# Conditioned linear attention on one core: opening, seam, end of the state and last stretch put in another order

## The chip, the cores and the metric

The kernel runs on one core of a Trainium2 chip. The metric is the device time of one execution in microseconds (us), as the median of several runs; a profile of one execution stands beside it. Five engines matter: TensorE (PE, matmuls, with its weight loads shown apart as PEld), VectorE (DVE), ScalarE (ACT), GpSimd (POOL) and SyncE (SP, which here only issues transfers). Each engine takes its own instructions strictly in the order in which they are written, and waits on semaphores for the others.

## What is computed

Two batches (b) of 2048 tokens with 512 channels, 8 heads of 64. The reference, cut to what matters:

```python
xn = _ln(x, ln_w, ln_b)
q = xn @ Wq + bq
k = xn @ Wk + bk + (1.0 - src_mask) * -1000000.0
q = softmax(q per head, over the 64 channels)
k = softmax(k, over the 2048 tokens)
v = ((xn @ Wv + bv) * src_mask)
att = einsum('bnhd,bnhl->bhdl', k, v)
y = einsum('bnhd,bhdl->bnhl', q, att)
scale, shift = split(silu(emb) @ W_emb + b_emb)
hh = _ln(y, ln2_w, ln2_b) * (1.0 + scale) + shift
return x + silu(hh) @ W_out + b_out
```

## The kernel before

A batch is T = 16 tiles of 128 tokens; tile m of the output counts through both batches, so batch 1 has the tiles 16 to 31 (written T to 2T-1). The order of each engine is written out by hand, as a list of calls; nothing reorders it. Every large product is made from three fp32r matmuls (high by high, high by low, low by high; `split_product`), four blocks of them to a tile, twelve matmuls in all. So each operand is split first: ACT copies the high part, DVE or POOL subtracts it for the low part.

Stages, in order of time:

- **Opening and first batch, keys and queries.** For each tile PE turns the normalised x (`turn_z`, four transposes into one PSUM bank ZB), ACT copies the high part out (`zT_high`), DVE the low part (`zT_low`), PE forms `product_k` and `product_q`. DVE adds the bias to k and keeps a running maximum (`k_tile`, two instructions), adds the bias to q (`q_add`), takes the maximum of each head (`q_top`), POOL subtracts it (`q_shift`), ACT takes the exponential (`exp_q`). The statistics of x go by chunks of tiles, listed in XC: `x_tile_stats` for each tile, then `x_finish` for a chunk, a chain of some 13 tiny DVE instructions (a reciprocal root by Newton steps, in four parts 0 to 3); only then can ACT normalise the tiles of the chunk (`normalise_x`). Weights are split too (`wk_high`, `weight_low`), and biases are worked out by `key_bias`, `bias_parts`, `bias_sum`.
- **State** (`state_steps`): PE accumulates `product_g` over 16 tiles in four banks; ACT and DVE prepare exponentials and masked x (`exp_k`, `ek_high`, `zm_high`, `k_less_max`, `masked_z`, `zm_low`, `ek_low`). Afterwards `sum_exponentials` (sums of the keys' exponentials), `products_att`, `att_blocks` give the attention matrix.
- **Seam and second batch.** The keys and queries of batch 1 are made while batch 0 goes through `product_y` (PE), `y_tile` (DVE, reciprocal and scaling, it frees the PSUM for the next `product_y`), `y_raw` and `y_finish` (statistics by the chunks YC, in four parts as above), `normalise_y` (ACT), `turn_y` (PE), `scale_shift` (ACT: four scalings and a tanh), `silu` (DVE), `h_high` (ACT), `h_low` (POOL), `product_out` (PE), `out_tile` (DVE), store (SP). Outputs up to HT-1 = 11 are done here; 12 to 15 are held for the state and the last stretch.
- **State of batch 1**, then the **last stretch**: `product_y` of tiles 16 to 31, their norms and outputs.

Two rules of the last stretch matter. `product_y(m)` waits for `y_tile(m-1)`. `product_out(m)` waits for `h_low(m)` and, since there are two output banks, for `out_tile(m-2)`. On ACT the loop is `scale_shift(m)`, `normalise_y(m+1)`, `h_high(m)`.

## Time and profile before

| | us |
|---|---|
| median of 3 runs (496.40 to 498.42) | 497.97 |
| the profiled execution | 496.72 |
| its span in the trace | 494.9 |
| PE busy | 465.5 (94%) |
| DVE busy | 364.5 (74%) |
| ACT busy | 265.0 (54%) |
| POOL busy | 124.6 (25%) |

Busy PE time counts from the start of a matmul to its modelled end, so overlapping matmuls count once. 1.8 us of the execution lie outside the span. Times in the rows below are microseconds from the start of the span.

### The profile page before, as it was taken

How to read it: one execution, taken by the hardware profiler on the slowest of the kernel's cores; microseconds unless marked ns; L12 is line 12 of the kernel's file. 1: busy time of each engine (PE TensorE's matmuls, PEld its weight loads, DVE VectorE, ACT ScalarE, POOL GpSimd, SP SyncE). 2: the span in 40 equal slices, each digit the busy share in tenths (PEclk: the TensorE clock that was granted, in tenths of full speed). 3: DMA queues.
4: the chain of work that ended last, by engine and by line, in shares of the span. 5: the costliest groups of instructions: out<-in, count | busy, mean ns of one | idle time of the engine just before them, and what ended most of it. 6: DMA issues, size and time to landing. Idle time of an engine off the chain costs nothing.

```text
span 494.9 us, 7296 instructions
## 1 busy us (share of the span) xinstructions
PE 465.5 (94%) x2478; PEld 370.4 (75%) x2478; DVE 364.5 (74%) x893; ACT 265.0 (54%) x487; POOL 124.6 (25%) x106
## 2 busy tenths in 40 slices
PE   4988999998899989999999999998899988999997
PEld 1666876885688768778888888887678857877765
DVE  6699976765878766879677568667998538777762
ACT  4234332321787323347556556656979635477782
POOL 0013311120100000104223333223310131456565
PEclk9999999999999999999999999999999999999999
DMA  8991110112132210110203212121321000333344
GB/s 280 360 373 51 44 42 3 43 48 101 45 126 85 86 34 10 44 42 1 86 22 128 85 44 86 44 85 67 106 88 63 1 0 23 121 103 118 127 152 147
DMA packets 23093, 43.50 MB, mean 88 GB/s; under 512 B 1992, under 2 KB 2064, under 8 KB 23056
## 3 DMA queue, kind: packets, MB, share of 16 engines
q1 hardware_dynamic: 21968, 40.93, 24.4%
q10 hardware_dynamic: 1088, 2.10, 1.1%
q8 instruction: 20, 0.33, 0.3%
q14 instruction: 17, 0.14, 0.1%
HBM read 34.64 MB, written 8.39 MB: 87 GB/s over the span
## 4 chain that ended last, share of the span: by engine, by line
PE 76%; DVE 15%; ACT 4%; issue 4%; DMA 1%; POOL 1%; DVEq 0%; ACTq 0%
PE ps L1067 20%; PE ps L1069 20%; PE ps L1068 20%; PE ps L1072 8%; PE ps L1228 4%; PE ps L1160 1%; ACT ps L394 1%; DVE kf L816 1%; DVE res L843 1%; DVE xst_raw L615 1%; ACT x_in L308 1%; DVE qs L716 1%; ACT kf L382 1%; PE ps L1213 1%; PE ps L1132 1%
## 5 line engine op out<-in xcount | busy, mean ns | idle before, releaser
L561 POOL TENSOR_TENSOR qs<-qs,qmax 128x512 f32<-128x512 f32 x32 | 35.9, 1121 | 199.0 <-DVE qmax L721 199.0
L1067 PE MATMUL ps<-wk_hi,zT_hi 128*128 128x512 f32 x128 | 53.7, 420 | 2.0 <-DVE kf L702 2.0
L1067 PE MATMUL ps<-ek_hi,zm_hi 128*128 128x512 f32 x128 | 50.8, 397 | 2.9 <-DVE ek_lo L757 2.1
L293 ACT ACTIVATE zT_hi<-ps 128x512 fp32r<-128x512 f32 x32 | 19.1, 597 | 64.2 <-PE ps L1072 64.1
L1067 PE MATMUL ps<-wq_hi,zT_hi 128*128 128x512 f32 x128 | 52.5, 411 | 0.3 <-DVE qs L716 0.3
L1068 PE MATMUL ps<-wk_lo,zT_hi 128*128 128x512 f32 x128 | 51.0, 398 | 0.0
L1069 PE MATMUL ps<-wk_hi,zT_lo 128*128 128x512 f32 x128 | 50.8, 397 | 0.0
L1069 PE MATMUL ps<-wq_hi,zT_lo 128*128 128x512 f32 x128 | 50.6, 395 | 0.0
L1068 PE MATMUL ps<-wq_lo,zT_hi 128*128 128x512 f32 x128 | 50.5, 395 | 0.0
L1069 PE MATMUL ps<-ek_hi,zm_lo 128*128 128x512 f32 x128 | 49.9, 390 | 0.0
L1068 PE MATMUL ps<-ek_lo,zm_hi 128*128 128x512 f32 x128 | 49.9, 390 | 0.0
L574 POOL TENSOR_TENSOR res<-res,bo_all 128x512 f32<-128x512 f32 x32 | 42.1, 1320 | 20.0 <-DMA res<-in_x_dram 10.7
L716 DVE TENSOR_TENSOR qs<-ps,bq_all 128x512 f32<-128x512 f32 x32 | 22.1, 689 | 32.0 <-PE ps L1069 29.9
L702 DVE SCALAR_TENSOR_TENSOR kf<-ps,pen,bk_all 128x512 f32<-128x512 f32 x32 | 23.9, 745 | 13.5 <-PE ps L1069 13.5
L695 DVE TENSOR_TENSOR zT_lo<-ps,zT_hi 128x512 fp32r<-128x512 f32 x32 | 21.9, 686 | 13.7 <-ACT zT_hi L293 13.7
L1067 PEld LDWEIGHTS ps<-ek_hi,zm_hi 128*128 128x128 f32 x128 | 24.0, 188 | 10.4 <-DVE ek_lo L757 3.6
L1067 PEld LDWEIGHTS ps<-wk_hi,zT_hi 128*128 128x128 f32 x128 | 24.4, 190 | 9.1 <-issue 3.4
L293 ACT ACTIVATE eqT<-ps 128x512 f32<-128x512 f32 x17 | 10.2, 600 | 38.2 <-PE ps L1072 38.2
L323 ACT ACTIVATE eq<-qs 128x512 f32<-128x512 f32 x32 | 20.0, 625 | 19.2 <-POOL qs L561 19.2
L747 DVE TENSOR_TENSOR zm_lo<-x_in,zm_hi 128x512 fp32r<-128x512 f32 x32 | 22.4, 701 | 10.4 <-PE ps L1069 9.4
L843 DVE TENSOR_TENSOR res<-ps,res 128x512 f32<-128x512 f32 x32 | 21.9, 683 | 10.8 <-PE ps L1069 7.2
L308 ACT ACTIVATE x_in<-x_in,x_shift,x_r 128x512 f32<-128x512 f32 x32 | 25.6, 806 | 6.9 <-DVE x_shift L647 6.9
(210 smaller groups left out, 1150.7 us busy)
## 6 DMA issues: line engine op xcount, KB each, us to landing
x_in<-in_x_dram SPq DMA_DIRECT2D x32, 512.0 KB, 3.5
res<-in_x_dram SPq DMA_DIRECT2D x32, 256.0 KB, 2.7
out_dram<-res SPq DMA_DIRECT2D x32, 256.0 KB, 2.0
y<-in_L_cond_Wk_dram ACTq DMA_DIRECT2D x2, 512.0 KB, 5.0
kf<-in_L_cond_Wq_dram ACTq DMA_DIRECT2D x1, 1024.0 KB, 7.8
eq<-in_L_cond_W_out_dram SPq DMA_DIRECT2D x1, 1024.0 KB, 9.1
wv_mod<-in_L_cond_Wv_dram SPq DMA_DIRECT2D x1, 1024.0 KB, 11.3
eq<-in_L_cond_W_emb_dram SPq DMA_DIRECT2D x4, 256.0 KB, 9.9
```

Source lines behind the costliest of these rows:

```text
L293: act.activation(o, i, ACT.Copy, scale=scale).then_inc(s[done], 1)
L308: act.activation(x_in[:, at, :], x_in[:, at, :], ACT.Identity, bias=x_shift[:, n:n + 1], scale=x_r[:, n:n + 1]).then_inc(s["z_ok"], 1)
L561: pool.tensor_tensor(q_heads, q_heads, qmax[:].unsqueeze(2).broadcast_to([P, H, DH]), ALU.subtract).then_inc(s["q_shift"], 1)
L574: pool.tensor_tensor(res[:, m % RR, :], res[:, m % RR, :], bo_all[:], ALU.add).then_inc(s["res_b"], 1)
L702: dve.scalar_tensor_tensor(out=kf[:, n, :], in0=ps[:, OB if m == 1 else KB, :], scalar=pen[:, m:m + 1], in1=bk_all[:], op0=ALU.add, op1=AL ...
L716: dve.tensor_tensor(qs[:], ps[:, TB if m == 1 else QB, :], bq_all[:], ALU.add).then_inc(s["q_sum"], 1)
L747: dve.tensor_tensor(zm_lo[:, n % LO, :], x_in[:, at, :], zm_hi[:, n % HI, :].bitcast(F32), ALU.subtract).then_inc(s["zm_lo_ok"], 1)
L843: dve.tensor_tensor(res[:, m % RR, :], o_bank(m), res[:, m % RR, :], ALU.add).then_inc(s["o_ok"], 1)
L1067: pe.matmul(o, a[0], bb[0], start=start, stop=False)
L1068: pe.matmul(o, a[0], bb[1], start=False, stop=False)
L1069: return pe.matmul(o, a[1], bb[0], start=False, stop=stop)
L1072: return pe.transpose(o, i, ident[0:i.shape[0], 0:i.shape[0]])
```

## The change

Nothing is computed in another way; instructions change places, one chunk of x's statistics is cut in two, one turn gets its own bank, and the last two tiles are normalised by DVE.

- **Opening.** The chunk (2, 6) of batch 0 becomes (2, 4) and (4, 6). The turn of tile 1 goes to bank YTB, so it needn't wait for the low part of tile 0; `normalise_x(0, 1)` and the turn move ahead of `product_k(0, 0)`; `key_bias(1)` ahead of the first turn. `turn_z(0, 2)` moves behind `product_q(0, 1)`. DVE's list is put in another order, and the masked scales (`x_masked`) go to the steps 10 to 15.
- **Seam and state.** `sum_exponentials` stands ahead of the last `product_g`, with ACT's copy of the sums ahead of the copies of g; the small products of the sums stand ahead of the attention products.
- **End of batch 1's loop and state.** `product_out(10)` ahead of the turn of the keys' maxima, `product_q(1, 15)` ahead of their spreading; `turn_y(13)` goes behind the second `product_g`; DVE's and ACT's lists follow.
- **Last stretch.** `product_out(12)` stands ahead of the attention products, `product_out(13)` and `(14)` between the first `product_y`. The tiles 18 and 19 are turned one step later, then two tiles at once; two `product_y` follow each of the outputs 16 and 17. DVE takes `silu` ahead of `out_tile`; the finishes of the last three chunks are cut in two halves.

```diff
-    XC = [[(0, 2), (2, 6), (6, 10), (10, 14), (14, 16)]] * 2
+    XC = [[(0, 2), (2, 4), (4, 6), (6, 10), (10, 14), (14, 16)], [(0, 2), (2, 6), (6, 10), (10, 14), (14, 16)]]
+    LATE = 2
...
+        def z_bank(m):
+            return ps[:, YTB if m == 1 else ZB, :]
...
             def state_steps(b, last=lambda n: None):
...
+                sums_out(b)
                 for j in (0, 2):
...
             normalise_x(0, 0)
+            normalise_x(0, 1)
             act.wait_ge(s["wk_in1"], 16)
             wk_high(2)
             zT_high(0, 0)
-            normalise_x(0, 1)
...
             for m in range(T + 2, 2 * T):
                 scale_shift(m)
-                if m + 1 < 2 * T:
+                if m + 1 < 2 * T - LATE:
                     normalise_y(m + 1)
                 h_high(m)
...
+            def normalise_late(m):
+                dve.wait_ge(s["y_norm"], nth_chunk(YC, m // T, m % T))
+                dve.tensor_scalar(y_of(m), y_of(m), y_r[:, m % SR:m % SR + 1], y_shift[:, m % SR:m % SR + 1],
+                                  ALU.mult, ALU.add).then_inc(s["yn_late"], 1)
...
             weight_low(wk_lo, wk_raw, wk_hi, "wk", 1)
+            weight_low(wk_lo, wk_raw, wk_hi, "wk", 2)
             zT_low(0, 0)
-            weight_low(wk_lo, wk_raw, wk_hi, "wk", 2)
             weight_low(wk_lo, wk_raw, wk_hi, "wk", 3)
             zT_low(0, 1)
+            weight_low(wq_lo, wq_raw, wq_hi, "wq", 0)
+            weight_low(wq_lo, wq_raw, wq_hi, "wq", 1)
+            x_tile_stats(0, 2)
+            x_tile_stats(0, 3)
+            weight_low(wq_lo, wq_raw, wq_hi, "wq", 2)
+            weight_low(wq_lo, wq_raw, wq_hi, "wq", 3)
+            x_finish(0, 1)
...
-            for f in range(NB):
-                weight_low(wq_lo, wq_raw, wq_hi, "wq", f)
-                x_tile_stats(0, 2 + f)
-            x_finish(0, 1)
...
             k_tile(0, 0)
+            x_tile_stats(0, 4)
+            x_tile_stats(0, 5)
             zT_low(0, 2)
+            k_tile(0, 1)
...
             q_add(0, 0)
             q_top(0, 0)
-            k_tile(0, 1)
...
-            x_part(0, 0)
+            x_finish(0, 2)
             q_add(0, 1)
             zT_low(0, 3)
             q_top(0, 1)
...
             q_top(0, 2)
+            x_part(0, 0)
             x_part(0, 1)
             x_part_end(0, 1)
-            x_masked(0, 0)
-            x_masked(0, 1)
             x_part_end(0, 2)
...
             state_steps(1, last_outputs)
+            out_tile(HT)
             att_blocks(1)
...
             silu(HT + 3)
             y_tile(T + 2)
             y_raw(T + 2)
-            out_tile(HT)
+            out_tile(HT + 1)
             y_tile(T + 3)
             y_raw(T + 3)
             silu(T)
             y_finish(T + 3)
+            out_tile(HT + 2)
             silu(T + 1)
-            out_tile(HT + 1)
             y_tile(T + 4)
             y_raw(T + 4)
-            out_tile(HT + 2)
-            y_tile(T + 5)
-            y_raw(T + 5)
-            y_tile(T + 6)
-            y_raw(T + 6)
             for m in range(T, 2 * T):
-                out_tile(m - 1)
                 if m + 2 < 2 * T:
                     silu(m + 2)
-                if m + 6 < 2 * T:
-                    y_finish(m + 6)
-                if m + 7 < 2 * T:
-                    y_tile(m + 7)
-                    y_raw(m + 7)
+                out_tile(m - 1)
+                if m >= T + 2 and m + 6 < 2 * T:
+                    y_finish(m + 6, (2, 3))
+                    if m + 6 == 2 * T - 1:
+                        for k in range(2 * T - LATE, 2 * T):
+                            normalise_late(k)
+                for k in (2 * m - T + 5, 2 * m - T + 6) if m < T + 2 else (m + 7,):
+                    if k < 2 * T:
+                        y_tile(k)
+                        y_raw(k)
+                        y_finish(k, (0, 1) if m >= T + 1 and k > T + 7 else range(4))
...
             key_bias(0)
+            key_bias(1)
             turn_z(0, 0)
-            key_bias(1)
+            turn_z(0, 1)
             product_k(0, 0)
-            turn_z(0, 1)
...
             key_bias(3)
+            product_k(0, 1)
             pe.wait_ge(s["wq_in"], 16)
             bias_parts(cols[:, LNB:LNB + NB], wq_raw, "bq_part")
-            product_k(0, 1)
             product_q(0, 0)
-            turn_z(0, 2)
...
             bias_sum("bq_ps")
             product_q(0, 1)
+            turn_z(0, 2)
...
             for n in range(T):
+                if n == T - 1:
+                    sum_exponentials(1)
                 product_g(1, n)
+                if n == 1:
+                    turn_y(HT + 1)
...
-            sum_exponentials()
+            product_out(HT)
             products_att(1)
...
             product_y(T)
             product_y(T + 1)
+            product_out(HT + 1)
             product_y(T + 2)
-            product_out(HT)
-            product_y(T + 3)
+            product_out(HT + 2)
             turn_y(T)
             turn_y(T + 1)
-            product_out(HT + 1)
+            product_y(T + 3)
+            product_out(HT + 3)
             product_y(T + 4)
-            product_out(HT + 2)
-            turn_y(T + 2)
-            product_y(T + 5)
-            product_out(HT + 3)
-            product_y(T + 6)
             for m in range(T, 2 * T):
                 product_out(m)
-                if m + 3 < 2 * T:
-                    turn_y(m + 3)
-                if m + 7 < 2 * T:
-                    product_y(m + 7)
+                for k in ((m + 2,), (m + 2,), (m + 2, m + 3))[m - T] if m < T + 3 else (m + 3,):
+                    if k < 2 * T:
+                        turn_y(k)
+                for k in (2 * m - T + 5, 2 * m - T + 6) if m < T + 2 else (m + 7,):
+                    if k < 2 * T:
+                        product_y(k)
```

## Rows read from the trace of the kernel before

**Rows 1.** Busy time by stretch of the span, all engines, granted clock, DMA share.

```profile
core 0: us, PE busy (x) PEld busy (x) DVE busy (x) ACT busy (x) POOL busy (x), PEclk, DMA share, GB/s
12.00:27.00 15.00, 13.48 (x56) 8.91 (x56) 10.58 (x33) 5.07 (x9) 0.00 (x0) 1.00 1.03 363
27.00:45.00 18.00, 16.76 (x78) 12.92 (x76) 16.40 (x45) 7.00 (x14) 4.41 (x4) 1.00 0.58 212
336.00:355.00 19.00, 15.96 (x84) 12.65 (x83) 16.62 (x23) 14.40 (x29) 7.57 (x6) 1.00 0.22 74
404.00:426.00 22.00, 17.87 (x106) 14.90 (x105) 17.84 (x58) 13.82 (x29) 2.62 (x3) 1.00 0.13 42
426.00:481.00 55.00, 51.49 (x285) 42.52 (x284) 40.92 (x124) 38.83 (x83) 33.05 (x26) 1.00 0.37 123
```

**Rows 2.** Whom PE waited for: us in total, times, longest.

```profile
PE ps L1228 <- DVE kf L816: 3.8, 4, 1.1
PE ps L1072 <- ACT kf L382: 3.5, 5, 0.9
```

**Rows 3.** Timeline, PE's first turn and first product: start, duration, instruction.

```profile
9.27 1.11 PE L1072 MATMUL ps<-ident,x_in 128*128 128x128 f32 x4 [1.23 <-ACT x_in L308]
12.39 0.63 PE L1068 MATMUL ps<-wk_lo,zT_hi 128*128 128x512 f32 x1
12.81 0.63 PE L1069 MATMUL ps<-wk_hi,zT_lo 128*128 128x512 f32 x1
14.59 0.39 PE L1068 MATMUL ps<-wk_lo,zT_hi 128*128 128x512 f32 x1
14.82 0.40 PE L1069 MATMUL ps<-wk_hi,zT_lo 128*128 128x512 f32 x1
```

**Rows 4.** Timeline of the opening: turn and low part of tile 2, then tile 4.

```profile
26.77 0.66 PE L1072 MATMUL ps<-ident,x_in 128*128 128x128 f32 x4 [1.52 <-ACT x_in L308]
28.09 0.69 DVE L695 TENSOR_TENSOR zT_lo<-ps,zT_hi 128x512 fp32r<-128x512 f32 x1 [0.75 <-ACT zT_hi L293]
...
42.93 0.68 DVE L695 TENSOR_TENSOR zT_lo<-ps,zT_hi 128x512 fp32r<-128x512 f32 x1
43.76 0.63 PE L1072 MATMUL ps<-ident,x_in 128*128 128x128 f32 x4 [0.63 <-DVE zT_lo L695]
45.36 0.47 PE L1067 MATMUL ps<-wk_hi,zT_hi 128*128 128x512 f32 x1 [0.97 <-DVE kf L702]
```

**Rows 5.** Timeline, seam; batch 1's keys' maxima; its second state tile.

```profile
182.50 0.63 PE L1072 MATMUL ps<-ident,x_in 128*128 128x128 f32 x4 [1.50 <-DVE zT_lo L695]
...
339.50 0.63 PE L1072 MATMUL ps<-ident,km 128*128 128x128 f32 x4 [1.56 <-DVE y L816]
...
354.38 0.50 PE L1067 MATMUL ps<-ek_hi,zm_hi 128*128 128x512 f32 x1 [1.32 <-DVE ek_lo L757]
```

**Rows 6.** Timeline, the first y of batch 1 and the first output after them.

```profile
404.70 1.13 PE L1228 MATMUL ps<-att,eq 128*128 128x130 f32 x8 [0.30 <-ACT eq L293]
406.95 1.13 PE L1228 MATMUL ps<-att,eq 128*128 128x130 f32 x8 [1.12 <-DVE kf L816]
```

**Rows 7.** Timeline of the last stretch: a finish of three tiles, one tile's chain.

```profile
431.25 0.18 DVE L631 BATCH_NORM_AGGREGATE ps<-yst_raw 128x2 f32<-128x6 f32 x1
434.09 0.21 DVE L812 RECIPROCAL rec<-ps 128x8 f32<-128x8 f32 x1
...
453.83 0.66 PE L1072 MATMUL ps<-ident,kf 128*128 128x128 f32 x4 [0.84 <-ACT kf L382]
456.04 0.60 ACT L399 ACTIVATE th<-ps 128x512 f32<-128x512 f32 x1
456.53 0.81 ACT L382 ACTIVATE kf<-kf,y_shift,y_r 128x512 f32<-128x512 f32 x1
457.00 0.68 DVE L843 TENSOR_TENSOR res<-ps,res 128x512 f32<-128x512 f32 x1
```

More of the change, by code:

```diff
@@ L315, in zT_high @@
                     act.wait_ge(s["q_ps"], m - 1)
-                copy(flat(zT_hi[:, n % 2]), ps[:, ZB, :], "zT_hi_ok")
+                copy(flat(zT_hi[:, n % 2]), z_bank(m), "zT_hi_ok")
             def exp_q(b, n):
@@ L902, in _ @@
             q_top(0, 1)
+            dve.tensor_tensor(lnb_w[:], cols[:, LNB:LNB + NB], cols[:, LNW:LNW + NB], ALU.subtract).then_inc(s["lnbw_ok"], 1)
             k_tile(0, 2)
@@ L915, in _ @@
                 x_part_end(0, n)
-                if n % NT == 3 and n // NT + 2 < len(XC[0]):
-                    x_masked(0, n // NT + 2)
+                if 10 <= n and n - 10 < len(XC[0]):
+                    x_masked(0, n - 10)
                 if n == T - 2:
@@ L1000, in _ @@
             masked_z(1, 0)
+            out_tile(HT - 2)
+            masked_z(1, 1)
+            zm_low(1, 0)
             k_less_max(1, 0)
-            out_tile(HT - 2)
             k_less_max(1, 1)
-            zm_low(1, 0)
             q_add(1, T - 1)
+            zm_low(1, 1)
             ek_low(1, 0)
             q_top(1, T - 1)
-            masked_z(1, 1)
+            ek_low(1, 1)
             k_less_max(1, 2)
             masked_z(1, 2)
-            silu(HT)
             out_tile(HT - 1)
-            zm_low(1, 1)
-            ek_low(1, 1)
             def last_outputs(n):
-                if n == 1:
+                if n == 0:
+                    silu(HT)
+                if n == 3:
                     silu(HT + 1)
-                if 3 <= n < 7:
-                    y_finish(T - 1, (n - 3,))
+                if 4 <= n < 8:
+                    y_finish(T - 1, (n - 4,))
                 if n == 10:
@@ L1077, in turn_z @@
                 pe.wait_ge(s["z_ok"], m + 1)
-                if m:
+                if m > 1:
                     pe.wait_ge(s["zT_lo_ok"], m)
                 for f in range(NB):
-                    last = turn(blk(ps[:, ZB, :], f), blk(x_in[:, at, :], f))
+                    last = turn(blk(z_bank(m), f), blk(x_in[:, at, :], f))
                 last.then_inc(s["zT_ps"], 1)
@@ L1154, in spread_kmax, with sum_exponentials @@
                 last.then_inc(s["kmax_ps"], 1)
-            def sum_exponentials():
+            def sum_exponentials(b):
+                pe.wait_ge(s["k_exp"], T * (b + 1))
                 for r in range(0, T, 4):
@@ L1204, in products_att @@
             def products_att(b):
+                pe.wait_ge(s["den_ok"], b + 1)
+                for q in range(NB):
+                    last = pe.matmul(ps[:, YB, 2 * q:2 * q + 2], blk(den, q), part[:, 0:2], start=True, stop=True)
+                last.then_inc(s["den_ps"], 1)
                 pe.wait_ge(s["gT_a"], 2 * b + 2)
@@ L1214, in products_att @@
                 last.then_inc(s["att_ps"], 1)
-                pe.wait_ge(s["den_ok"], b + 1)
-                for q in range(NB):
-                    last = pe.matmul(ps[:, YB, 2 * q:2 * q + 2], blk(den, q), part[:, 0:2], start=True, stop=True)
-                last.then_inc(s["den_ps"], 1)
             def product_y(m):
@@ L1310, in _ @@
             for n in range(T):
+                if n == T - 1:
+                    sum_exponentials(0)
                 product_g(0, n)
-            sum_exponentials()
             pe.wait_ge(s["pick_ok"], 1)
```

43 lines of the change are left out of this document (22 added, 21 removed).

## The prediction

> **What bounds the kernel now.** I read the busy time by stretch first [rows 1]. PE is busy for nearly all of the steady parts; what a new order can win is PE's lost time, in four places: the opening (1.5 us idle from 12 to 27, 1.2 from 27 to 45), the step into the state of batch 1 (3.0 from 336 to 355), the first y of the last stretch (4.1 from 404 to 426) and the rest of it (3.5 from 426 to 481). The list of PE's waits [rows 2] names the causes in the last stretch: `product_y` waiting for `y_tile`, 3.8 us in four waits, and `turn_y` waiting for `normalise_y`, 3.5 in five. A wait costs more than its length: from one y to the next stand 2.25 us [rows 6], the y alone takes 0.9 of PE (1.13 less the drain), so 1.35 is lost where the list says 1.12. I add 0.24 to each listed wait. PE's work is not changed by the reordering, so the change is worth what it alters in this lost time. Between 45 and 336 the orders are the same but for a few tiny instructions under PE's work; I cost them at nothing, and 0.3 if a DVE wait for k comes later by them.
>
> PE's prices: a product is twelve matmuls of 0.23 us step [rows 3], so 2.8; a turn 0.4; a y 0.9.
>
> **Opening.** Before the change the first products run with a step of 0.42 us (1.2 GHz, the lower level) and then of 0.23 (2.4 GHz) [rows 3], while the granted clock in the rows is 1.00 throughout. With `key_bias(1)` and two turns ahead of the first product PE is busy without a gap from its first matmul, so I expect the first product at the fast step: 0.9 won. It starts at about 12.0, since one more `weight_low` (0.7) stands ahead of `zT_low(0, 0)` on DVE. Then PE runs without a wait: product 2.8, small turn 0.2, two key biases 2.0, product 2.8, bias parts 1.0, product 2.8, bias sum 0.9, product 2.8, which is 15.3, to 27.3. Only here stands `turn_z(0, 2)`: turn and copy take 1.3 (26.77 to 28.09) [rows 4], and `zT_low(0, 2)` starts at 28.6, against 28.09 before. But it is queued on DVE ahead of `k_tile(0, 1)`, the bias of q, `q_add(0, 0)` and everything behind: DVE stands idle for some 5 us, and PE waits 1.4 for its low part before it can turn tile 3.
>
> From there DVE sets the pace. Before, it needed from `zT_low(0, 2)` at 28.09 to `zT_low(0, 4)` at 42.93, 14.8 us, nearly all busy (16.4 of 18 in [rows 1]). After, the same instructions stand between the two, plus a second `x_finish`: 2.84 for three tiles [rows 7], for two and with the overlap 2.65. The masked scales (0.3) leave, and of DVE's idle time in that stretch (1.6) I let 0.5 go. So `zT_low(0, 4)` starts at 28.6 + 14.8 + 1.8 = 45.2, 2.3 later. PE, which before waited 0.63 for it and then 0.97 for `k_tile(0, 3)` behind it [rows 4], is later by the same. **Opening: +2.3.** Bounds: 0 if DVE's extra finish falls into a gap that I don't see, +3.5 if the first product stays slow and DVE keeps its idle time.
>
> **Seam.** `sum_exponentials` moved ahead of the last `product_g` takes cover from the copies of g, but the condition columns and the sums (1.9 + 1.0) still cover them in batch 0. DVE's two finishes (2.65 and 2.85) now start after the last g, 3.6 us later, and end at about 181.4, just ahead of `zT_low(1, 0)`, whose result PE's next turn awaits at 182.5 [rows 5]. I take 0, between -0.2 and +0.5. That turn's wait of 1.5 stays, since the second bank is for tile 1 of batch 0 alone. In batch 1 `product_out(12)` gives the cover; y(16) gains 0.1.
>
> **Into the state of batch 1.** Two waits go: 1.56 at the turn of the maxima, now covered by `product_out(10)`, and 1.32 at the second `product_g` [rows 5], with 0.24 each, and a small one of 0.4 at the first: -3.8. Three come. The maxima are spread 1 us later, so `silu(11)` and `product_out(11)` start later: 0.65. `zm_low(1, 1)` waits for `product_out(11)` to end, and now `ek_low(1, 0)` is queued behind it, so the first `product_g` waits for two DVE instructions after that product: 1.45. Its last block waits for `out_tile(11)`, further back on DVE: 0.75. **Together -0.9**, between -2 and +1.
>
> **Last stretch.** Times as if y(16) still started at 404.70 [rows 6].
>
> - Won: the waits at the second to fourth y (1.12, 1.11, 0.48, with 0.24 each: 3.4), filled by held outputs. The first, y(16) to y(17), stays. The turn waits of [rows 2] go too (3.5 and 5 x 0.24: 4.7): three of them come when a finish of 2.84 (431.25 to 434.09) [rows 7] blocks DVE's `silu`, and the halves are 1.55 and 1.3; the others from ACT, which loses two `normalise_y`. **-8.1.**
> - `turn_y(16)` and `(17)` come before ACT has normalised the tiles: +0.5.
> - `product_out(16)` needs `out_tile(14)`, now queued behind `y_finish(19)`: `silu(16)` at 418, finish 2.8, `out_tile` 0.7, so 422.3. PE is through with y(20) at 420.1: +2.2.
> - `turn_y(18)` now stands behind `product_out(16)`, and DVE has `silu(18)` ahead of `out_tile(15)` and `y_tile(21)`. From the start of a turn to the end of its tanh are 2.81 (453.83 to 456.64) [rows 7]; then `silu` 0.65, `out_tile` 0.65, `y_tile` 1.05: 5.15, before PE may start y(22). PE has only the turn and y(21) to do, 1.3: **+3.8**. The next pair, y(23) and y(24) behind `silu(19)`, is the same: **+3.8**.
> - `turn_y(20)` and `turn_y(21)` stand back to back, but ACT normalises tile 21 after `scale_shift(20)`, which needs the first turn: turn to normalised tile is 457.34 - 453.83 = 3.5 [rows 7], less 0.4 for the turn: **+3.1**.
> - Behind them `silu` ahead of `out_tile` makes an output wait for the chain turn, scale, tanh, `silu`, `out_tile`: 2.81 + 0.65 + 0.7 = 4.15 against 3.2 of PE (a turn and a product) when no y stands between: twice 0.6 at the chunks with a finish, 3.2 in the last six tiles, where no y is left, and 0.5 for the last load of x. **+4.9.**
>
> Sum: -8.1 + 0.5 + 2.2 + 3.8 + 3.8 + 3.1 + 4.9 = **+10.2**. Bounds: +6 if half of the small ones is hidden, +12.
>
> **The whole.** 2.3 + 0 - 0.1 - 0.9 + 10.2 = +11.5 on the profiled execution, 496.7 + 11.5 = 508.2. That execution lies 1.25 under the median, so the median would be 509.5 by the same sum; I forecast between them, **508.5**.
>
> **A rule that speaks against the change.** The longest wait of PE behind its first product is 1.6 us in this trace [rows 5], and the step after it is still the fast one; the three new waits of 3 to 4 us are longer than any that it shows, so it can't say what follows them. The Trainium skill, "TensorE: Matmul & The Clock Gate", section "HAM oscillation — how this bites in real kernels", says that idle time between bursts can put the array back to its half clock, so that the next burst starts slow. By that rule the sum would be larger.
>
> **Rivals.**
>
> 1. *The clock falls in the long waits.* Each return to the lower level costs the difference of the steps, 0.42 - 0.23, on some matmuls [rows 3]; in the opening the slow stretch ran from 9.27 to about 14, and half of that, 2.4, was lost. For one to three of the new waits: +2 to +6, **512.5**. For it: their length. Against it: the wait of 1.5 in the opening [rows 4] doesn't do it. 0.12.
> 2. *The large waits are there, but the rest is better than I count.* The finish in halves and the early `silu` give DVE and ACT enough room that the later waits (4.9) mostly vanish, and the opening costs under 1: 11.5 - 4 - 1.5 = +6, **503.5**. 0.14.
> 3. *Faster: the covers work.* All listed waits of the last stretch go (-8.1), into the state another -0.9, the opening -1. The point is `y_tile(21)`: if the scale and tanh of tile 18 were over by the time DVE reaches `silu(18)`, y(22) would start 1.4 after y(21) and the three large waits (10.7) would not exist; with the small ones kept that gives -3 to -8, **491**. Against it: the turn of 18 stands behind `product_out(16)` in PE's list, and the chain behind it is 2.8 us in the rows. 0.08.
> 4. *It does nothing measurable*, what it wins and loses being equal, which needs two of the three large waits wrong: **498**. 0.05.
>
> **Chances.** The forecast 0.61 (its own range 505 to 511.5), rivals 0.12, 0.14, 0.08, 0.05. The range takes in the forecast and the first two: **502 to 513**, which leaves out the last two and some of the ends. A measurement of this kernel can tell about 0.5% from no change: faster 0.08, the same 0.05, slower 0.87.
>
> **What would show it.** In the profile after: PE's steady turns of the opening start 2 us later (tile 5's turn near 46 instead of 43.76), with DVE idle from 23 to 28.6; no wait at the second `product_g` of batch 1; from the first y of batch 1 on, waits of PE of 3.5 or so at y(22) and y(24), of `product_y` for `y_tile`, and one of 3 at the turn of tile 21, for `normalise_y`; DVE idle ahead of `silu(18)` and `silu(19)`, released by ACT's tanh. I am wrong if these three aren't there, or if the steps after them are 0.42 instead of 0.23.

## The result, and the profile after

| | before | after |
|---|---|---|
| median, us | 497.19 (of 4) | 516.74 (of 4, 516.08 to 518.96) |
| the profiled execution | 496.72 | 516.87 |
| its span | 494.9 | 515.0 |

The changed kernel is slower, by a factor of 1.0405 (95% interval 1.0377 to 1.0434): 19.6 us. The forecast was 508.5, its range 502 to 513. The direction was right, the size was not: 8 us more were lost than the sum said.

Busy times by stretch, the same columns as in [rows 1]. The first two lines are the opening. The work behind it comes later in the changed kernel, so its windows are moved: 341 to 360 has the step into the state of batch 1 (336 to 355 in [rows 1]), 414 to 436 the first y of the last stretch (404 to 426), 436 to 491 the rest of it (426 to 481). The last line is the window 426 to 481 as it stands, for a comparison further down.

```profile
core 0: us, PE busy (x) PEld busy (x) DVE busy (x) ACT busy (x) POOL busy (x), PEclk, DMA share, GB/s
12.00:27.00 15.00, 14.44 (x60) 9.29 (x59) 10.94 (x31) 5.78 (x10) 0.00 (x0) 1.00 1.00 358
27.00:45.00 18.00, 13.87 (x59) 10.72 (x58) 14.37 (x36) 6.13 (x11) 4.39 (x4) 0.91 0.61 224
341.00:360.00 19.00, 15.27 (x79) 12.00 (x78) 14.79 (x23) 12.95 (x26) 6.39 (x5) 1.00 0.13 43
414.00:436.00 22.00, 18.45 (x106) 15.21 (x105) 16.02 (x54) 11.16 (x23) 5.36 (x5) 1.00 0.15 49
436.00:491.00 55.00, 43.50 (x238) 36.83 (x236) 37.78 (x114) 33.57 (x70) 23.89 (x19) 0.94 0.27 87
426.00:481.00 55.00, 42.33 (x229) 35.87 (x228) 37.07 (x118) 31.89 (x67) 21.65 (x17) 0.94 0.26 86
```

Against [rows 1] PE's idle time falls from 12 to 27 (0.6 us, before 1.5) and at the first y (3.6, before 4.1). It grows from 27 to 45 (4.1, before 1.2) and at the step into the state (3.7, before 3.0), and in the rest of the last stretch it is 11.5 of 55, where it had been 3.5. And a number that was 1.00 in every line of before is 0.91 and 0.94 here: the granted clock.

Whom PE waited for (us in total, times, longest), to be held against [rows 2]:

```profile
PE ps L1247 <- DVE kf L823: 8.2, 3, 3.6
PE ps L1085 <- DVE res L855: 6.3, 5, 2.2
PE ps L1090 <- DVE zT_lo L702: 5.5, 4, 1.9
...
PE ps L1090 <- ACT kf L388: 3.1, 2, 2.9
```

The longest wait behind the first product is 3.6 us instead of 1.6. Here are those of the opening and of the last stretch in the timeline of PE (the number in brackets is the idle time just before):

```profile
30.58 0.63 PE L1090 MATMUL ps<-ident,x_in 128*128 128x128 f32 x4 [1.50 <-DVE zT_lo L702]
...
38.73 0.63 PE L1090 MATMUL ps<-ident,x_in 128*128 128x128 f32 x4 [1.93 <-DVE zT_lo L702]
...
47.83 0.63 PE L1090 MATMUL ps<-ident,x_in 128*128 128x128 f32 x4 [0.56 <-DVE zT_lo L702]
...
416.92 1.13 PE L1247 MATMUL ps<-att,eq 128*128 128x130 f32 x8 [1.12 <-DVE kf L823]
...
432.72 0.47 PE L1085 MATMUL ps<-wo_hi,zT_hi 128*128 128x512 f32 x1 [2.15 <-DVE res L855]
...
440.65 1.13 PE L1247 MATMUL ps<-att,eq 128*128 128x130 f32 x8 [3.56 <-DVE kf L823]
...
449.47 2.07 PE L1247 MATMUL ps<-att,eq 128*128 128x130 f32 x8 [3.56 <-DVE kf L823]
...
458.22 0.66 PE L1090 MATMUL ps<-ident,kf 128*128 128x128 f32 x4 [2.90 <-ACT kf L388]
```

The four large waits of the forecast are all there: 2.15 at `product_out(16)`, 3.56 at y(22) and again at y(24), 2.90 at the turn of tile 21; the outputs behind them wait 0.50, 1.37 and twice 0.28. What made the wait at y(22) can be read on DVE, and it is the chain that the forecast named, tanh, `silu`, `out_tile`, `y_tile`:

```profile
438.37 0.69 DVE L849 SCALAR_TENSOR_TENSOR th<-th,ps 128x512 f32<-128x512 f32 x1 [3.62 <-ACT th L405]
438.97 0.69 DVE L855 TENSOR_TENSOR res<-ps,res 128x512 f32<-128x512 f32 x1
...
439.81 0.69 DVE L823 TENSOR_TENSOR kf<-ps,rec 128x512 f32<-128x512 f32 x1
```

DVE stands idle for 3.62 us ahead of `silu(18)`, while the y(21) that it would have to scale was finished on PE at 437.1, 2.5 us before `y_tile(21)` starts.

**Where the 20.1 us of span are.** I follow PE's same instructions in both traces. The shift is +3.8 when the opening is over (the matmul at 113.72 before starts at 117.52 after, that at 133.25 at 137.05), +5.3 at the second turn of batch 1 (182.50 in [rows 5], 187.79 after), +10.0 at the first y (404.70 in [rows 6], 414.67 after), of which 2.8 is `product_out(12)`, work that is only done earlier. From there to the end are 100.3 us after and 90.2 before; with these 2.8 the last stretch has lost 12.9. So: opening 3.8, seam 1.5, state of batch 1 1.9, last stretch 12.9.

**The clock.** PE's products after the waits of the opening:

```profile
40.06 0.77 PE L1085 MATMUL ps<-wk_hi,zT_hi 128*128 128x512 f32 x1 [0.70 <-DVE kf L709]
40.62 0.63 PE L1086 MATMUL ps<-wk_lo,zT_hi 128*128 128x512 f32 x1
41.05 0.63 PE L1087 MATMUL ps<-wk_hi,zT_lo 128*128 128x512 f32 x1
...
43.15 0.39 PE L1086 MATMUL ps<-wk_lo,zT_hi 128*128 128x512 f32 x1
43.38 0.39 PE L1087 MATMUL ps<-wk_hi,zT_lo 128*128 128x512 f32 x1
```

From 40.62 to 43.15 the step from one matmul to the next is 0.42 us, then 0.23 again. In the windows the granted clock of such stretches is half of the full one, 1.2 GHz; there are five of them, called slow stretches from here on, and their steps slow steps:

```profile
40.00:43.00 3.00, 2.94 (x7) 2.42 (x8) 2.74 (x4) 2.44 (x5) 0.74 (x2) 0.50 0.00 0
183.00:186.00 3.00, 3.00 (x38) 2.77 (x32) 2.15 (x14) 1.26 (x2) 0.00 (x0) 0.51 0.02 5
360.00:364.00 4.00, 4.00 (x13) 3.10 (x12) 2.74 (x5) 3.42 (x6) 0.99 (x1) 0.57 0.74 264
449.00:453.00 4.00, 3.53 (x13) 3.22 (x14) 2.37 (x5) 0.00 (x0) 2.17 (x2) 0.57 0.41 131
460.00:463.00 3.00, 3.00 (x8) 2.32 (x8) 2.68 (x13) 1.69 (x4) 1.31 (x2) 0.51 0.38 130
```

Before has none behind its first products. The mean granted clock of the span is 0.983: 0.017 of 515 us is 8.8 us, the most that the slow stretches can have cost; what overlapped waiting cost nothing. The first of the five is such a case, as the part on why the prediction was wrong shows.

### The profile page after: what moved, and what is told of

Same layout as the page of the kernel before. It is cut to its first block, busy times and chain, and to the rows that moved or that the text cites. A ratio compares the mean times of both kernels' runs of the same rounds, so it can differ in the third digit from the quotient of the medians.

```text
span 515.0 us, 7311 instructions
## 1 busy us (share of the span) xinstructions
PE 473.4 (92%) x2478; PEld 377.2 (73%) x2478; DVE 366.9 (71%) x911; ACT 264.0 (51%) x485; POOL 123.6 (24%) x106
## 4 chain that ended last, share of the span: by engine, by line
PE 80%; DVE 10%; ACT 3%; issue 3%; POOL 2%; DMA 2%; POOLq 0%; ACTq 0%; SPq 0%; DVEq 0%
PE ps L1085 21%; PE ps L1087 20%; PE ps L1086 20%; PE ps L1090 8%; PE ps L1247 5%; PE ps L1179 1%; PE ps L1131 1%; DVE res L855 1%; DMA y<-in_L_cond_Wk_dram 1%; DVE kf L823 1%; ACT ps L400 1%; PE ps L1236 1%; POOL qs L568 1%; PE ps L1150 1%; DVE yst_raw L622 1%
## 5 line engine op out<-in xcount | busy, mean ns | idle before, releaser
L400 ACT ACTIVATE ps<-ps,ab 128x128 f32<-128x128 f32 x64 | 23.6, 429 | 15.8 <-PE ps L1090 15.5
L754 DVE TENSOR_TENSOR zm_lo<-x_in,zm_hi 128x512 fp32r<-128x512 f32 x32 | 22.4, 701 | 12.9 <-PE ps L1087 12.2
```

Source lines behind the costliest of these rows:

```text
L400: act.activation(blk(u_of(m), f), blk(yt_bank(m), f), ACT.Identity, bias=ab[:, m // T, 1, f:f + 1], scale=ab[:, m // T, 0, f:f + 1]).then_ ...
L754: dve.tensor_tensor(zm_lo[:, n % LO, :], x_in[:, at, :], zm_hi[:, n % HI, :].bitcast(F32), ALU.subtract).then_inc(s["zm_lo_ok"], 1)
```

## Experiments

The theory: PE's new waits cost what they last, and stretches at the lower clock come on top. The rivals differ from part to part, and each expectation names its own. The first four kernels each make one part of the change alone, on the kernel before.

**The opening alone (e1_open)**

```diff
+    XC = [[(0, 2), (2, 4), (4, 6), ...], [(0, 2), (2, 6), ...]]
...
             key_bias(0)
-            turn_z(0, 0)
             key_bias(1)
+            turn_z(0, 0)
+            turn_z(0, 1)
             product_k(0, 0)
...
-            turn_z(0, 2)
...
             product_q(0, 1)
+            turn_z(0, 2)
```

> The kernel before with the new opening alone (XC, bank, order on PE, ACT, DVE). Theory A (waits of PE and on top of them the lower clock after the longest): +3 to +4.5, about 501, with a stretch of 0.42 us steps behind the turn of tile 4. Rival B (only the longer DVE queue, the slow steps in the changed kernel having come from elsewhere): +2.3, 499.5, all steps 0.23. Rival C (the opening is the part that pays, the loss is all behind it): 497 or less.

Measured: 501.99 (501.05 to 503.38), 1.0096 of before (1.0069 to 1.0123), so +4.8 us for the part that I had put at +2.3. In the profiled execution 2.3 us of the delay are no matter of the order: the weights for PE's first matmuls landed at 8.30, and at 5.99 in the profile of before. In its trace PE waits:

```profile
39.96 0.63 PE L1080 MATMUL ps<-ident,x_in 128*128 128x128 f32 x4 [1.93 <-DVE zT_lo L698]
...
49.05 0.63 PE L1080 MATMUL ps<-ident,x_in 128*128 128x128 f32 x4 [1.92 <-DVE zT_lo L698]
```

The wait of 1.93 at 39.96 was not followed by slow steps this time, so PE came to the turn of tile 5 earlier and waited 1.92 there (0.56 in the changed kernel); behind it and the 0.69 came the slow steps, 50.93 to 53.49. DVE sets the pace here, as forecast, and the clock falls at one turn or the other: behind the first in the changed kernel, behind the second here and in three later kernels with this opening (f1_fill, f2_silu, g1_turn).

**The sums ahead of the last state tile, alone (e2_sums)**

```diff
             for n in range(T):
+                if n == T - 1:
+                    sum_exponentials(0)
                 product_g(0, n)
-            sum_exponentials()
```

> The kernel before with the sums alone moved: sum_exponentials ahead of the last product_g of either batch, ACT's copy first, the small products of the sums ahead of the attention products. No wait of PE should come or go by it. Theory A (the 1.5 us that the seam lost are slow matmul steps, brought by a run of small matmuls that no full product interrupts): +1.5, 498.7, with the attention products taking 2.6 instead of 2.1 us. Rival B (the slow steps there came by chance of where the opening had shifted them): 0, 497.2.

Measured: 497.43 over ten executions, 1.0012 (0.9995 to 1.003). Nothing, as the sum said, and no slow stretch at the seam:

```profile
182.00:188.00 6.00, 6.00 (x31) 4.97 (x32) 3.65 (x9) 1.90 (x3) 0.00 (x0) 1.00 0.28 90
```

So this edit alone did not bring the slow stretch of the changed kernel at 183 to 186, in this execution; its one slow stretch stands at 408 to 412. With the whole change f1_fill and g1_turn (below) have the one at the seam too, f2_silu hasn't. Other executions show one near that place in code that is as before (below).

**The new step into the state of batch 1, alone (e3_entry)**

```diff
+            turn_kmax(1)
             product_q(1, T - 1)
+            spread_kmax(1)
...
             zm_low(1, 0)
+            k_less_max(1, 0)
+            k_less_max(1, 1)
             q_add(1, T - 1)
+            zm_low(1, 1)
             ek_low(1, 0)
...
             out_tile(HT - 1)
-            zm_low(1, 1)
-            ek_low(1, 1)
```

> The kernel before with the new step into the state of batch 1 alone. Theory A (out_tile(11) waits for POOL's bias of its residual, which is queued behind the shift of the last q, itself behind q_top on DVE; a wait of 2 us in the first product_g and slow steps after it): +1 to +2, 498.7. Rival B (my sum for this step, with 0.75 there and no slow steps): -0.9, 496.3.

Measured: 498.88, 1.0024 (1.0004 to 1.0045): a small loss in place of my gain of 0.9. The first `product_g` waits 1.46 for `ek_low`, the 1.45 of the forecast, and its last block:

```profile
353.36 0.62 PE L1071 MATMUL ps<-ek_hi,zm_hi 128*128 128x512 f32 x1 [1.97 <-DVE res L846]
```

This should have been 0.75. Behind it the slow steps run from 353.36 to 356.77. The cause of the 1.97 stands in the changed kernel, on DVE and POOL:

```profile
355.64 1.42 POOL L568 TENSOR_TENSOR qs<-qs,qmax 128x512 f32<-128x512 f32 x1 [5.21 <-DVE qmax L728]
357.02 1.44 POOL L581 TENSOR_TENSOR res<-res,bo_all 128x512 f32<-128x512 f32 x1
...
358.57 0.69 DVE L855 TENSOR_TENSOR res<-ps,res 128x512 f32<-128x512 f32 x1 [1.23 <-POOL res L581]
```

`out_tile(11)` isn't late by its place on DVE: DVE stands idle for 1.23 us and waits for POOL's `add_bias(11)`, which is queued behind the last `q_shift`; and that waits for `q_top`, which the change puts behind one more call on DVE, `zm_low(1, 1)`, and this one waits for PE to end `product_out(11)`. POOL had been idle for 5.21 us before.

**The same, with POOL's bias ahead of its last shift (f3_bias)**

```diff
                     h_low(HT - 1)
+                    add_bias(HT - 1)
                 q_shift(1, t)
-            add_bias(HT - 1)
```

> The kernel before with the new step into the state of batch 1, and POOL's bias of tile 11 put ahead of its last q_shift. Theory A (the wait of 1.97 us in the first product_g is out_tile(11) waiting for that bias, queued behind the shift): the wait falls to 0.8 or less, the slow steps behind it go, 496.5. Rival B (out_tile(11) is late by DVE's own queue): the wait stays near 2, 498.9.

Measured: 497.37, 0.9996 (0.9973 to 1.0018). The wait of 1.97 is gone, and the one at the first `product_g` is longer:

```profile
349.52 0.50 PE L1071 MATMUL ps<-ek_hi,zm_hi 128*128 128x512 f32 x1 [1.91 <-DVE ek_lo L760]
```

That settles the cause of the 1.97: POOL's queue. What it is worth, about 1.4 us by the two ratios, comes with overlapping intervals; the two waits were 3.43 together and are 1.91. Theory A was wrong on the clock: slow steps are there too, from 350.79 to 353.95, now behind the 1.91. This entry in its mended form costs nothing and wins nothing.

**The new last stretch alone (e4_last)**

```diff
             product_out(HT)
             products_att(1)
...
             product_y(T + 1)
+            product_out(HT + 1)
             product_y(T + 2)
-            product_out(HT)
-            product_y(T + 3)
+            product_out(HT + 2)
...
             for m in range(T, 2 * T):
-                out_tile(m - 1)
                 if m + 2 < 2 * T:
                     silu(m + 2)
+                out_tile(m - 1)
```

> The kernel before with the new last stretch alone (product_out(12) behind the sums, ahead of the attention products). Theory A (waits of 2.2, 3.6, 3.6 and 2.9 us and two stretches of slow steps behind them): +12 to +14, 510. Rival B (the waits without the slow steps): +10, 507. Rival C (the parts are not additive, the last stretch costs less when nothing before it was shifted): under +8.

Measured: 513.89 (512.37 to 514.85), 1.0335 (1.0301 to 1.037): this part alone is most of the loss.

```profile
427.22 0.47 PE L1074 MATMUL ps<-wo_hi,zT_hi 128*128 128x512 f32 x1 [2.15 <-DVE res L850]
...
435.15 2.07 PE L1235 MATMUL ps<-att,eq 128*128 128x130 f32 x8 [3.56 <-DVE kf L818]
...
446.45 1.24 PE L1235 MATMUL ps<-att,eq 128*128 128x130 f32 x8 [3.56 <-DVE kf L818]
...
455.26 0.66 PE L1079 MATMUL ps<-ident,kf 128*128 128x128 f32 x4 [2.90 <-ACT kf L384]
```

To the hundredth the waits of the changed kernel: they come from the order, not from the time at which the stretch starts. This time both waits of 3.56 were followed by slow steps (437.44 to 440.43, 447.91 to 450.47), and two more slow stretches lie in code that is as before:

```profile
182.00:185.00 3.00, 3.00 (x10) 2.44 (x10) 2.32 (x5) 0.60 (x1) 0.00 (x0) 0.58 0.43 154
355.00:359.00 4.00, 4.00 (x12) 3.13 (x11) 3.17 (x6) 3.90 (x7) 0.00 (x0) 0.57 0.36 138
```

They stand behind the waits of 1.50 and 1.32 of [rows 5], which in the profile of before had no such effect. The four parts measure +4.8, +0.6, +1.2 and +16.7 us (each ratio less one, by its own median of before), 23.3 together, and the whole +20.1 by the same reckoning (19.6 between its two medians). The parts don't add up to better than 3 us; the slow stretches and the landing of the weights differ between executions by as much.

**The changed kernel with PE kept busy in the three long waits (f1_fill)**

```diff
+            def filler(count):
+                for _ in range(count):
+                    pe.matmul(ps[:, TB, :], wo_hi[:, 0, 0:P], wo_hi[:, 0, :], start=True, stop=True)
...
+                    if k == T + 5:
+                        filler(8)
                     if k < 2 * T:
                         turn_y(k)
...
+                    if k in (T + 6, T + 8):
+                        filler(10)
```

Nobody reads what these matmuls write.

> The changed kernel with matmuls that nobody reads put into its three longest waits: ten ahead of product_y(22), ten ahead of product_y(24), eight ahead of turn_y(21), 0.23 us each, into a free PSUM bank. They delay nothing, since PE waits there 3.6, 3.6 and 2.9 us. Theory A (PE's idle time in these waits brings the lower clock behind them): no slow steps behind these three, 1.7 us won for each of the two slow stretches there, 513.3 against 516.7; what is left of the waits is 1.2, 1.2 and 1.0. Rival B (the slow steps are not from idle time, or the clock looks at something else than whether PE computes): 516.7, slow steps as before.

Measured: 514.52 (512.84 to 518.34), 1.0332 (1.0305 to 1.0359): 2.2 us less than the changed kernel between the medians (3.6 by the two ratios, whose intervals don't touch), though PE does more work. The waits for the same releasers shrink from 3.56, 3.56 and 2.90 to 1.27, 1.24 and 1.05, the dependences stay, and the clock holds in the last stretch:

```profile
426.00:481.00 55.00, 48.06 (x269) 39.67 (x267) 38.84 (x121) 33.70 (x71) 23.03 (x18) 1.00 0.26 83
```

against 0.94 in the changed kernel. This separates the two costs of one wait: the time to the releaser, which a filler can't shorten, and the slow steps behind it, which did not come here. It is one profiled execution, and the wait at y(22) had none in the changed kernel either, so the medians carry the proof more than the trace. The profiled execution, the slowest of the four, has a slow stretch of 5.1 us (50.08 to 55.20) in the opening, one at the seam (185 to 189) and one at the step into the state of batch 1.

**The changed kernel with `silu(18)` and `silu(19)` behind the y tiles (f2_silu)**

```diff
             for m in range(T, 2 * T):
-                if m + 2 < 2 * T:
+                if T + 2 <= m and m + 2 < 2 * T:
                     silu(m + 2)
...
+                if m < T + 2:
+                    silu(m + 2)
             out_tile(2 * T - 1)
```

> The changed kernel with DVE's silu(18) and silu(19) put behind the two y_tiles of their step instead of ahead of out_tile. Theory A (the wait of y(22) and y(24) is DVE standing in front of silu until ACT's tanh of the tile turned late): the wait at y(22) falls from 3.6 to 1.1, that at y(24) to about 2.7, since the finish of tile 22 stands in front of it, the wait at the turn of 21 stays 2.9; -3.4 by the waits, and -1.7 more if one slow stretch goes with them: 511.6 to 513.3. Rival B (the y tiles are late for another reason, the PSUM or PE): nothing changes, 516.7.

Measured: 510.62 (510.31 to 513.41), 1.0277 (1.0249 to 1.0305): 6.1 us of the loss come back by two calls moved, by the medians.

```profile
436.94 1.13 PE L1249 MATMUL ps<-att,eq 128*128 128x130 f32 x8 [1.12 <-DVE kf L823]
...
444.93 1.13 PE L1249 MATMUL ps<-att,eq 128*128 128x130 f32 x8 [2.73 <-DVE kf L823]
...
452.16 0.66 PE L1092 MATMUL ps<-ident,kf 128*128 128x128 f32 x4 [2.90 <-ACT kf L388]
```

and by stretch, with the granted clock behind the five busy times:

```profile
425.00:481.00 56.00, 46.07 (x268) 39.15 (x268) 42.04 (x127) 37.19 (x79) 26.54 (x21) 1.00 0.31 102
```

The waits fall by 2.44 and 0.83, 3.3 us together, and the two slow stretches of the last stretch are gone in this execution. From y(16) to PE's last matmul are 90.5 us here and 96.2 in the changed kernel: 5.7 less, so some 2.7 of it are the slow steps, when the small waits, 0.3 longer here, are counted too. The slow stretch of the seam is missing as well; the ones in the opening and at the step into the state of batch 1 are there. The wait of 2.90 is untouched and is followed by no slow steps here.

**The same, with ACT normalising tile 21 before it scales tile 20 (g1_turn)**

```diff
             for m in range(T + 2, 2 * T):
+                if m == T + 4:
+                    normalise_y(m + 1)
                 scale_shift(m)
-                if m + 1 < 2 * T - LATE:
+                if m != T + 4 and m + 1 < 2 * T - LATE:
                     normalise_y(m + 1)
```

> The kernel with silu(18) and silu(19) moved back (510.6), and besides ACT's normalise_y(21) ahead of scale_shift(20). Theory A (turn_y(21), written directly behind turn_y(20), waits because ACT normalises 21 only behind the scaling that needs the turn of 20): the wait of 2.9 us there goes, 507 to 508. Rival B (tile 21 is late by its statistics, the finish of the chunk on DVE): the wait stays, 510.6.

Measured: 512.7 (511.29 to 514.16), 1.0306 (1.0274 to 1.0338): no faster than f2_silu, although the wait that it aims at has gone from 2.90 to 0.52:

```profile
452.91 0.66 PE L1094 MATMUL ps<-ident,kf 128*128 128x128 f32 x4 [0.52 <-ACT kf L388]
...
456.32 0.47 PE L1089 MATMUL ps<-wo_hi,wk_hi 128*128 128x512 f32 x1 [1.85 <-DVE res L857]
```

and on DVE `silu(20)`:

```profile
454.88 0.69 DVE L851 SCALAR_TENSOR_TENSOR th<-th,ps 128x512 f32<-128x512 f32 x1 [3.39 <-ACT th L405]
```

`product_out(20)` now waits 1.85 for `out_tile(18)`, which is queued behind `silu(20)` on DVE, and that waits for the tanh of tile 20. From the first turn of the pair to that product are 4.53 us here (451.79 to 456.32) and 4.80 in f2_silu (448.66 to 453.46): 0.27 won of a wait of 2.90. So the 3.1 at this place in my sum has two causes that end at nearly the same time, and either alone makes nearly all of it. In this execution slow steps stand behind the new wait (457.09 to 460.47).

**A second turn early without DVE's new order (f4_open)**

On the kernel before: `key_bias(1)` and the turn of tile 1 in its own bank ahead of the first product, `product_k(0, 1)` ahead of the bias parts; besides these, ACT's `normalise_x(0, 1)` and DVE's third `weight_low` move ahead and DVE's copy of the columns moves back; the chunk of four stays whole, and `turn_z(0, 2)` keeps its place ahead of the bias sum.

```diff
             key_bias(0)
-            turn_z(0, 0)
             key_bias(1)
-            product_k(0, 0)
+            turn_z(0, 0)
             turn_z(0, 1)
+            product_k(0, 0)
```

> The kernel before with the useful half of the new opening: key_bias(1) and the turn of tile 1 (own bank) ahead of the first product, the copy of the second columns behind the finish; the chunk (2, 6) stays whole, turn_z(0, 2) stays ahead of the bias sum, DVE's order else as before. Theory A (what the opening lost is the split chunk's second finish and DVE standing at zT_low(0, 2)): DVE starts on the weights of q 4 us earlier, the low part of tile 4 comes 2.5 to 3 us earlier, 494.5, if the transfers of x and the weights are there in time. Rival B (turning tile 1 early is itself the loss): 497.5 or more.

Measured: 497.68 over twelve executions, 1.0001 (0.9987 to 1.0015).

```profile
43.15 0.63 PE L1075 MATMUL ps<-ident,x_in 128*128 128x128 f32 x4 [2.11 <-DVE zT_lo L698]
...
44.74 0.61 PE L1070 MATMUL ps<-wk_hi,zT_hi 128*128 128x512 f32 x1 [0.97 <-DVE kf L705]
```

PE's wait at the turn of tile 2, 1.52 in [rows 4], is gone, and that turn starts 2.05 us earlier (24.72). The wait at the turn of tile 5 has grown from 0.63 to 2.11, so most of the gain is given back some 18 us later, where DVE's list is the bound, and slow steps follow (44.74 to 48.13).

**The same with PE kept busy there (g2_open)**

```diff
+                if n == 4:
+                    filler(6)
                 if n + 1 < T:
                     turn_z(0, n + 1)
+                if n == 4:
+                    filler(3)
```

> The mended opening (497.7), with matmuls that nobody reads in PE's wait for the low part of tile 4 (six of 0.23 us ahead of turn_z(0, 5), three behind it). Theory A (the 2 us that the mended opening wins are paid back by slow steps behind that wait): no slow steps near 45 us, 495.8. Rival B (it wins nothing because the weights' transfers set its start): 497.7 or more.

Measured: 497.6, 1.0004 (0.9986 to 1.0021). The waits fall from 2.11 to 1.31 and from 0.97 to 0.27, and the clock in the window is 1.00:

```profile
40.00:50.00 10.00, 8.41 (x38) 6.30 (x37) 9.45 (x32) 2.45 (x4) 2.31 (x2) 1.00 0.17 52
```

The slow steps of the opening are gone, but this execution has two such stretches elsewhere (182.80 to 184.48 and 355.07 to 358.44, in code as before), and the median doesn't move.

**`silu` ahead of `out_tile` on the kernel before, for seven tiles (g3_silu), and both (g4_both)**

```diff
             for m in range(T, 2 * T):
+                if T + 2 <= m <= T + 8:
+                    silu(m + 2)
                 out_tile(m - 1)
-                if m + 2 < 2 * T:
+                if m + 2 < 2 * T and not T + 2 <= m <= T + 8:
                     silu(m + 2)
```

> The kernel before with DVE's silu(m+2) ahead of out_tile(m-1) for m = 18 to 24 only, where the turn has long been made and y still follow. Theory A (silu first is sound where its tanh is ready, and shortens the way to the next turn): the three waits of 0.85 us at the turns shrink, 496.3. Rival B (silu first costs out_tile what it gives, as in the changed kernel): 497.5 or more.

> The two last ones together, as the version meant to beat both kernels. If they add: 494.7. If the slow steps come up elsewhere by the shift in time: 496 to 497.5.

Measured: g3_silu 496.3, 0.9987 (0.9967 to 1.0006); g4_both 496.22 (494.4 to 501.44), 0.9981 (0.9952 to 1.0009). g4_both is g2_open, with its unread matmuls, and g3_silu together. Neither can be told from before. What may pay is `silu` first where a y stands between: of the five waits of [rows 2] for `kf` of ACT only two of over 0.45 us are left in g4_both (0.86 and 0.66). Among executions with a mean granted clock of 1.0, the six of before in the same comparison took 496.51 to 497.02, the three of g3_silu 496.03 to 496.14, the three of g2_open 495.70 to 496.95, and the three of g4_both 494.40, 494.94 and 495.21. By these `silu` first is worth about 0.7 us alone and the two together about 2; but this picks executions by their clock after the fact, and over all executions the difference drowns.

## Why the prediction was wrong in size, step by step

The step that failed is the clock: the sum had no term for slow steps, which stood as a rival with 0.12, and they cost 5.8 of the 8.6 us that were missing from it. The rest is a wait for POOL that was put at 0.75 and was 1.97, and in the opening a transfer that landed 1.0 later and a stretch of DVE that was put at 16.6 and took 17.26.

| part | forecast | measured | the difference |
|---|---|---|---|
| opening | +2.3 | +3.8 | weights 1.0 later, DVE's stretch 0.7, 0.2 less elsewhere; slow steps 0 |
| seam | 0 | +1.5 | slow steps |
| state of batch 1 | -0.9 | +1.9 | POOL's queue 1.2, slow steps 1.5, 0.1 not placed |
| last stretch, with y(16) | +10.1 | +12.9 | slow steps, about 2.8 |
| sum | +11.5 | +20.1 | slow steps 5.8, others 2.8 |

At the step into the state of batch 1 the slow steps are counted as the matmuls at 0.42 (eight) times the 0.19 by which they exceed 0.23; at the seam and in the last stretch they are what is left when the forecast terms are taken off. The seam is borne out by f2_silu, which has no slow stretch there: from the wait of 1.00 in the steady part to the second turn of batch 1 are 68.84 us in it (117.71 to 186.55), 68.78 in before (113.72 to 182.50) and 70.27 in the changed kernel, so the forecast of 0 held but for them. In the last stretch y(24) and the three matmuls behind it take 3.15 us from 449.47 to 452.62 where they take 1.7 at the fast step, and the matmuls from 459.53 to 462.66 lose 1.4.

The last stretch can also be counted from the waits in the two traces, with the 0.24 for each. What was to go was 8.1 and is 8.1; the four large waits were to be 12.9 and are 13.1; the small ones were to be 5.4 and are 3.8 in the list (0.16, 0.50, 1.37, 0.28, 0.28) with 0.6 more behind PE's last matmul, where the last residual comes late. With 2.8 of slow steps that is 12.2 of the 12.9; the other 0.7 isn't placed. So that the rest came to the forecast 10.1 is in part luck: its small terms were about 1 too large, and what isn't placed made up for it.

**Right: what bounds, and the three large waits.** The form of the sum held. Its terms for the last stretch were 2.2, 3.8, 3.8 and 3.1, and with my 0.24 for each the list gives 2.39, 3.80, 3.80 and 3.14. The turn waits and the y waits that were to go did go, and y(17) kept its 1.12. f2_silu shows the named cause by undoing it. Rival 3, that DVE reaches `silu(18)` after the tanh, is refuted by DVE's 3.62 of idle time there. Rival 2 had the smaller later waits right in direction, by about 1 of its 4 us, and the opening wrong.

**Wrong: the clock.** My own test was "or if the steps after them are 0.42 instead of 0.23", and they are. Rival 1 had the mechanism and a chance of 0.12. It failed in two ways. It looked for slow stretches behind the three waits of 3 to 4 us alone, one to three of them; of the five, two stand behind such waits (3.56, 2.90), two behind shorter ones (1.93 with 0.70, and 1.97), and one behind no long wait at all. And it was made a rival, where it belonged in the sum. My argument against it was that the waits of 1.5 in before do nothing. That was one execution, and a lucky one: of the 29 executions of before that stand beside the last four kernels only six have a mean clock of 1.0; the others go down to 0.992. The mean clock alone doesn't say what that costs, since it depends on where the slow stretches fall: the six took 496.51 to 497.02, the nine with 0.996 no longer, 495.90 to 497.19, but the three with 0.997 took 498.24 to 499.04, and the seven with 0.992 or 0.993 took 497.31 to 500.66. The sum stood on the profile of an execution without slow stretches, with no term for them.

The Trainium skill, "TensorE: Matmul & The Clock Gate", section "HAM oscillation — how this bites in real kernels", has idle time between bursts put the array back to its half clock, so that each burst starts slow. The traces agree in kind for four of the five slow stretches of the changed kernel, which come with or behind waits of 1.93 to 3.56 us; the fifth, at the seam, has no idle time of PE in the 3 us before it. What they add is that it came behind some waits of a given length and not behind others.

**Wrong: a queue that was not looked at.** For `out_tile(11)` I counted DVE's queue (0.75). Its other operand comes by POOL, whose last `q_shift` waits for a DVE instruction that the change moves back. The wait was 1.97. The prediction costed what was moved on DVE and not what POOL had queued behind it.

**Opening.** The wait at the turn of tile 3 was to be 1.4 and is 1.50; DVE was to stand idle for some 5 us and does so for 6.03; the first product runs at the fast step, as forecast, and starts at 13.01 instead of 12.0, because the weight transfer on which the first matmul waits landed at 6.99 and not at 5.99 as in before. In other executions it landed at 5.83, 5.95, 7.45 and 8.30: this scatter belongs to no order. The turn of tile 5 was to be near 46 and is at 47.83: 1.0 by the landing, and 0.7 because DVE took 17.26 us from `zT_low(0, 2)` (29.74) to `zT_low(0, 4)` (47.00) where the sum had 16.6.

The slow steps of the opening (40.62 to 43.15, seven of them, 1.3 us of PE's time) cost the changed kernel nothing. DVE's 17.26 is the same, within 0.01, in e1_open, f1_fill, f2_silu and g1_turn, where no slow step falls between those two calls, and PE's turn of tile 5 waits for DVE in all five: 0.56 behind the slow steps, 1.92 to 1.95 without. The slow steps only took the place of waiting. What the order itself costs can be read in f2_silu, where the weights landed at 5.96, as in before: its first product matmul behind that turn starts at 48.04, in before at 45.36 [rows 4], 2.7 later and not 2.3. There the slow steps come behind the turn, and are paid: 4.0 later at 117.71.

**A fault of the method of adding.** In g1_turn a wait of 2.90 could be taken away for 0.27, since another chain of nearly the same length ends at the same place. A forecast term for a wait that is *added* is less exposed to this; a term for one *removed* must be the difference to the second longest.

**Left open.** Why one wait is followed by slow steps and its twin is not, and why the seam has a slow stretch in the changed kernel, f1_fill and g1_turn with no wait just ahead of it, where PE does only short matmuls. What the slow stretches cost is shown; that idle time of PE brings them is borne out by the three filled waits and not proved. No version was found that clearly beats the kernel before.

## What to carry to other kernels

Where an order is written out by hand, a call that is moved ahead of another on one engine moves everything behind it back to the time at which *its* last operand is there; look at that operand's chain first, on all engines, POOL's queue too. Count a new wait of PE twice, once for its length and once for the steps at the lower clock that may follow it (about 1.5 us each here, behind some waits and not behind others of the same length, and nothing where PE would next have waited for another engine anyway), and read the mean granted clock of several executions before you call the profiled one typical. Unread matmuls in a wait that can't be avoided gave back 2 us here, but undoing the wait gave 6.

## What the runs showed of the hardware

- A slow stretch lasts 1.7 to 3.4 us of steps at 0.42 in most cases (5.1 in f1_fill and 5.5 in g1_turn, both in the opening), and the shorter ones cost up to about 1.5 us of PE's time; the one in the opening of the changed kernel cost PE 1.3 and the kernel nothing.
- The same wait isn't always followed by one. The 3.56 at y(22): not in the changed kernel, but in e4_last. The 1.50 at the seam: not in before, but in e4_last and g2_open. The 1.93 at the turn of tile 4: in the changed kernel, but not in e1_open, f1_fill, f2_silu or g1_turn. The 2.90 at the turn of tile 21: in the changed kernel, but not in e4_last or f2_silu. The 1.97 at the step into the state of batch 1 (1.95 to 1.97): in all five kernels that have it. The 2.15 at `product_out(16)`: in none of the five. The second of the waits of 1.12 at the first y: in e1_open, e2_sums, f3_bias and f4_open (at 408 to 415), in code that is as before, and not in the profile of before.
- At the seam the granted clock fell to 0.51 from 183 to 186 while PE had been busy for all of the 3 us before, with the small matmuls of the attention products (64 of them in 2.64 us):

```profile
181.75 2.64 PE L1236 MATMUL ps<-wv_mod,y 128*64 128x64 f32 x64
```

```profile
180.00:183.00 3.00, 3.00 (x59) 2.98 (x60) 2.55 (x20) 0.25 (x1) 0.00 (x0) 1.00 0.00 0
```
